# Searching the 6,249th largest score two bits at a time instead of one

## The reference, cut to what matters

```python
def _L1_ffn_ref(x, attention_mask, wr, br, w1, b1, w2, b2):
    b, s, d = x.shape                      # here 1, 12500, 256
    weights = (jnp.einsum('bsd,do->bso', x, wr) + br)[..., 0]
    k = max(1, int(CAPACITY * s))          # CAPACITY = 0.5: 6250
    kk = k - 1 if k > 1 else 1             # 6249
    _, idx = jax.lax.top_k(weights, k)
    sel_idx = idx[:, :kk]
    sel = jnp.take_along_axis(x, sel_idx[:, :, None], axis=1)
    h = jax.nn.gelu(jnp.einsum('bkd,dh->bkh', sel, w1) + b1)
    y = jnp.einsum('bkh,hd->bkd', h, w2) + b2
    y = y * jnp.take_along_axis(weights, sel_idx, axis=1)[..., None]
    processed = jnp.zeros_like(x).at[batch_idx, sel_idx].set(y)
    return processed + x
```

## Time and profile before

| | |
|---|---|
| median of 3 runs | 8393.51 us |
| lowest, highest | 8387.45, 8396.27 us |
| the profiled execution: its time | 8392.08 us |
| the profiled execution: its span | 8390.3 us |
| busy PE / PE weight loads / DVE / ACT / POOL | 77% / 58% / 42% / 23% / 46% |
| mean granted TensorE clock | 0.868 of full speed |
| instructions | 109,810 |

### The profile page before, as it was taken

How to read it: one execution, slowest core, us unless ns; L and a number is a source line. 1 busy time by engine, 2 the same in 40 slices (tenths; PEclk the granted TensorE clock), 3 DMA queues, 4 the chain that set the end, 5 groups by cost and what they waited for, 6 DMA issues and landing times. The chain is left out here.

```text
span 8390.3 us, 109810 instructions
## 1 busy us (share of the span) xinstructions
PE 6473.1 (77%) x28541; PEld 4831.1 (58%) x28542; DVE 3545.2 (42%) x8238; ACT 1915.5 (23%) x4350; POOL 3823.0 (46%) x3997
## 2 busy tenths in 40 slices
PE   3797887778876899576578888785488877798699
PEld 2555555555555677463266666564366665577677
DVE  3211123333333322333345555555666655577620
ACT  1123430000011122121022222221012334465121
POOL 1567777777774000067777777774200000000231
PEclk9898878898886799758889998897799999899599
DMA  5776769999982100267677777775477766564520
GB/s 162 253 243 225 226 230 343 346 340 344 337 303 87 53 20 21 53 209 238 218 246 243 240 240 240 238 242 153 142 237 238 225 204 195 181 203 160 175 73 17
DMA packets 604940, 1708.05 MB, mean 204 GB/s; under 512 B 109370, under 2 KB 334479, under 8 KB 515140
## 3 DMA queue, kind: packets, MB, share of 16 engines
q1 hardware_dynamic: 338260, 981.33, 34.0%
q0 software_dynamic: 190752, 655.07, 24.6%
q10 hardware_dynamic: 75764, 69.93, 2.8%
HBM read 1084.38 MB, written 624.00 MB: 204 GB/s over the span
## 5 line engine op out<-in xcount | busy, mean ns | idle before, releaser
L723 POOL DMA_INDIRECT rows_ring<-h_rows,src_idx x1660 | 1726.3, 1040 | 653.0 <-issue 505.3
L1839 POOL DMA_INDIRECT x_sb<-xn_rows,src_tile x1563 | 1526.5, 977 | 470.7 <-issue 449.0
L2610 PE MATMUL sums_ps_sum<-x_sb,sums_weighted 128*125 x4124 | 1003.5, 400 | 264.1 <-DVE sums_weighted L2574 162.2
L816 PE MATMUL agg_ps_sum<-agg_rows,agg_sel_w 128*128 128x257 f32 x3080 | 996.6, 472 | 271.0 <-DMA agg_rows<-edge_rows 185.2
L2610 PEld LDWEIGHTS sums_ps_sum<-x_sb,sums_weighted 128*125 128x125 f32 x4124 | 786.0, 196 | 481.5 <-issue 352.2
L2574 DVE SCALAR_TENSOR_TENSOR sums_weighted<-x_sb 128x125 f32 x2062 | 720.0, 349 | 539.8 <-PE sums_ps_sum L2610 385.4
L816 PEld LDWEIGHTS agg_ps_sum<-agg_rows,agg_sel_w 128*128 128x128 f32 x3080 | 532.4, 217 | 513.3 <-issue 375.1
L792 DVE TENSOR_TENSOR agg_sel<-iota,dst_item 128x1280 bf16<-128x1280 f32 x166 | 249.9, 1505 | 878.5 <-PE agg_ps_sum L817 875.3
L2540 POOL DMA_INDIRECT node_tops<-tops,last_edge x98 | 93.1, 950 | 1127.1 <-DMA x_sb<-row_lots 1109.7
L2642 ACT ACTIVATE sums_z<-sums_ps_sum 125x257 f32<-125x257 f32 x500 | 193.0, 386 | 864.2 <-PE sums_ps_sum L2610 764.0
L2131 PE MATMUL mix_ps_h<-mix_x1t,mix_w 128*128 128x256 f32 x1600 | 384.4, 396 | 0.7 <-ACT mix_x1t L2193 0.7
(11 more groups left out here) (555 smaller groups left out, 11085.8 us busy)
## 6 DMA issues: line engine op xcount, KB each, us to landing
row_lots<-x_sb SPq DMA_DIRECT2D x195, 1048.0 KB
x_sb<-row_lots SPq DMA_DIRECT2D x195, 1048.0 KB
edge_rows<-rows_ring POOLq DMA_DIRECT2D x154, 1290.0 KB
agg_rows<-edge_rows SPq DMA_DIRECT2D x154, 1290.0 KB
sums<-sums_z ACTq DMA_DIRECT2D x500, 125.5 KB
fin_z<-sums SPq DMA_DIRECT2D x97, 642.5 KB, 3.8
xn_turned<-norm_xt SPq DMA_DIRECT2D x150, 256.0 KB, 2.0
rows_ring<-h_rows,src_idx POOLq DMA_INDIRECT x1660
```

The lines of the kernel that those rows point to most:

```text
L723: pool.indirect_dma_start(self.ring[:, s, i, :], None, self.table, bass.IndirectOffsetOnAxis(g.src_idx[:, item:item + 1], 0)).then_inc(sel ...
L816: pe.matmul(ps[:, bass.ds(off, W)], sel_w[:, u, j, :], tiles[:, j, 0:W], start=False, stop=False, skip_group_check=True)
L1839: pool.indirect_dma_start(self.ring[:, s, i, :], None, g.xn_rows, bass.IndirectOffsetOnAxis(g.src_tile[:, tile:tile + 1], 0)).then_inc(sel ...
L2610: pe.matmul(ps[0:M, bass.ds(bank, SW)], weighted[:, s + j, :, :].rearrange("p n w -> p (n w)"), rows[:, bass.ds(off, SW)], start=False, st ...
```

## The change

The search takes two bits a step. Three candidates (digit 1, 2 and 3 at the two bits under test) are compared in a row, each with its own column of `cnt`; one matmul sums the three columns; the largest digit whose total is at least `need` is or-ed into `cur`. The steps go from 31 to 16 (the last has one bit left: its digits are 0, 1 and 1). The conditional copy and the bare semaphore increment go; a reduction to the maximum and one more "or" come in. The candidates of the next step are formed at the end of a step, so the first ones are a copy ahead of the loop, and three constants are set instead of one. The diff, its declarations cut:

```diff
-        hit = ph.sb("hit", [P, TILES])
-        cnt = ph.sb("cnt", [P, 1])
+        hit = ph.sb("hit", [P, 3, TILES])
+        cnt = ph.sb("cnt", [P, 3])
...
-        BITS = 31
+        STEPS = 16
...
-                with pe.Fori(0, BITS + 2) as k:
-                    pe.wait_ge(counted, k + 1)
+                pe.wait_ge(counted, 1)
+                pe.matmul(ps_c[:, 0:1], g.ones[:, :], cnt[:, 0:1], start=True, stop=True).then_inc(summed, 1)
+                with pe.Fori(0, STEPS) as k:
+                    pe.wait_ge(counted, 3 * k + 4)
                     pe.matmul(ps_c[:, :], g.ones[:, :], cnt[:, :], start=True, stop=True).then_inc(summed, 1)
...
-                done(dve.memset(bit[:, :], 1 << (BITS - 1)))
+                for d in range(3):
+                    done(dve.memset(digit[:, d:d + 1], (d + 1) << 29))
                 done(dve.memset(cur[:, :], 0))
+                done(dve.tensor_copy(cand[:, :], digit[:, :]))
                 base = n.n
 
-                with dve.Fori(0, BITS) as k:
-                    m = Count(base + 3 * k)
-                    dve.tensor_tensor(cand[:, :], cur[:, :], bit[:, :], ALU.bitwise_or).then_inc(step, 1)
+                with dve.Fori(0, STEPS) as k:
+                    m = Count(base + 5 * k)
+                    for d in range(3):
+                        dve.tensor_scalar(hit[:, d, :], um[:, :], cand[:, d:d + 1].bitcast(F32), 0.0, ALU.is_ge, ALU.add,
+                                          accum_out=cnt[:, d:d + 1]).then_inc(counted, 1)
+                    dve.wait_ge(summed, k + 2)
+                    dve.scalar_tensor_tensor(won[:, :], ps_c[:, :], need[:, 0:1], digit[:, :], ALU.is_ge, ALU.mult).then_inc(step, 1)
                     dve.wait_ge(step, m.up())
-                    dve.tensor_scalar(hit[:, :], um[:, :], cand[:, :].bitcast(F32), 0.0, ALU.is_ge, ALU.add, accum_out=cnt[:, :]).then_inc(counted, 1)
-                    dve.wait_ge(summed, k + 2)
-                    dve.tensor_scalar(ok[:, :], ps_c[:, :], need[:, 0:1], None, ALU.is_ge).then_inc(step, 1)
+                    dve.tensor_reduce(best[:, :], won[:, :], AX, ALU.max).then_inc(step, 1)
+                    dve.tensor_scalar(digit[:, :], digit[:, :], 2, None, ALU.logical_shift_right).then_inc(step, 1)
+                    dve.wait_ge(step, m.up(2))
+                    dve.tensor_tensor(cur[:, :], cur[:, :], best[:, :], ALU.bitwise_or).then_inc(step, 1)
                     dve.wait_ge(step, m.up())
-                    dve.sem_inc(ok_seen, 1)
-                    dve.copy_predicated(cur[:, :], ok[:, :], cand[:, :])
-                    dve.tensor_scalar(bit[:, :], bit[:, :], 1, None, ALU.logical_shift_right).then_inc(step, 1)
+                    dve.tensor_tensor(cand[:, :], cur[:, :].to_broadcast([P, 3]), digit[:, :], ALU.bitwise_or).then_inc(step, 1)
                     dve.wait_ge(step, m.up())
```

More of the change, by code:

```diff
@@ L2895, in select @@
     with phase(nc, "sel") as ph:
-        loaded, counted, summed, step, rank_done, ok_seen, stored = (
-            ph.sem(s) for s in ("loaded", "counted", "summed", "step", "rank_done", "ok_seen", "stored"))
+        loaded, counted, summed, step, rank_done, stored = (
+            ph.sem(s) for s in ("loaded", "counted", "summed", "step", "rank_done", "stored"))
         br = ph.sb("br", [P, 1])
@@ L2900, in select @@
         um = ph.sb("um", [P, TILES])
-        hit = ph.sb("hit", [P, TILES])
-        cnt = ph.sb("cnt", [P, 1])
+        hit = ph.sb("hit", [P, 3, TILES])
+        cnt = ph.sb("cnt", [P, 3])
         sign = ph.sb("sign", [P, 1])
         need = ph.sb("need", [P, 1])
-        ok = ph.sb("ok", [P, 1], I32)
-        bit = ph.sb("bit", [P, 1], I32)
+        won = ph.sb("won", [P, 3], I32)
+        best = ph.sb("best", [P, 1], I32)
+        digit = ph.sb("digit", [P, 3], I32)
         cur = ph.sb("cur", [P, 1], I32)
-        cand = ph.sb("cand", [P, 1], I32)
+        cand = ph.sb("cand", [P, 3], I32)
         thr = ph.sb("thr", [P, 1])
@@ L2913, in select @@
         run = ph.sb("run", [P, TILES])
-        ps_c = ph.psum("c", [P, 1])
+        ps_c = ph.psum("c", [P, 3])
         ps_in = ph.psum("in", [P, TILES])
         ps_tot = ph.psum("tot", [P, TILES])
-        BITS = 31
+        STEPS = 16
         with nc.Block() as block:
@@ L2929, in _ @@
             def _(pe):
-                with pe.Fori(0, BITS + 2) as k:
-                    pe.wait_ge(counted, k + 1)
+                pe.wait_ge(counted, 1)
+                pe.matmul(ps_c[:, 0:1], g.ones[:, :], cnt[:, 0:1], start=True, stop=True).then_inc(summed, 1)
+                with pe.Fori(0, STEPS) as k:
+                    pe.wait_ge(counted, 3 * k + 4)
                     pe.matmul(ps_c[:, :], g.ones[:, :], cnt[:, :], start=True, stop=True).then_inc(summed, 1)
-                pe.wait_ge(counted, BITS + 3)
+                pe.wait_ge(counted, 3 * STEPS + 2)
+                pe.matmul(ps_c[:, 0:1], g.ones[:, :], cnt[:, 0:1], start=True, stop=True).then_inc(summed, 1)
+                pe.wait_ge(counted, 3 * STEPS + 3)
                 pe.matmul(ps_in[:, :], g.upper[:, :], eq[:, :], start=True, stop=True)
@@ L2949, in _ @@
                 done(dve.tensor_tensor(w[:, :], w[:, :], g.maskbias[:, :], ALU.add))
-                dve.tensor_scalar(hit[:, :], w[:, :], 0.0, 0.0, ALU.is_ge, ALU.add, accum_out=cnt[:, :]).then_inc(counted, 1)
+                dve.tensor_scalar(hit[:, 0, :], w[:, :], 0.0, 0.0, ALU.is_ge, ALU.add, accum_out=cnt[:, 0:1]).then_inc(counted, 1)
                 dve.wait_ge(summed, 1)
-                done(dve.tensor_scalar(sign[:, :], ps_c[:, :], float(KEEP), None, ALU.is_ge))
+                done(dve.tensor_scalar(sign[:, :], ps_c[:, 0:1], float(KEEP), None, ALU.is_ge))
                 done(dve.tensor_scalar(need[:, :], sign[:, :], float(2 * KEEP - NODES - 1), float(NODES - KEEP + 1), ALU.mult, ALU.add))
@@ L2974, in _ @@
                     dve.wait_ge(step, m.up())
-                n = Count(base + 3 * BITS)
+                n = Count(base + 5 * STEPS)
                 done(dve.tensor_scalar(thr[:, :], cur[:, :].bitcast(F32), sign[:, 0:1], None, ALU.mult))
                 dve.tensor_scalar(eq[:, :], w[:, :], thr[:, 0:1], None, ALU.is_equal)
-                dve.tensor_scalar(gt[:, :], w[:, :], thr[:, 0:1], 0.0, ALU.is_gt, ALU.add, accum_out=cnt[:, :]).then_inc(counted, 1)
-                dve.wait_ge(summed, BITS + 2)
@@ L2980, in _ @@
-                done(dve.tensor_scalar(need[:, :], ps_c[:, :], -1.0, float(KEEP), ALU.mult, ALU.add))
+                dve.tensor_scalar(gt[:, :], w[:, :], thr[:, 0:1], 0.0, ALU.is_gt, ALU.add, accum_out=cnt[:, 0:1]).then_inc(counted, 1)
+                dve.wait_ge(summed, STEPS + 2)
+                done(dve.tensor_scalar(need[:, :], ps_c[:, 0:1], -1.0, float(KEEP), ALU.mult, ALU.add))
                 dve.sem_inc(counted, 1)
```

## The result

The changed kernel takes 8361.82 us in the median of nine runs (8341.08 to 8370.81), the kernel before 8384.15 in nine runs beside it (8375.49 to 8396.27). The ratio is 0.997 with a 95% interval of 0.996 to 0.998, so 22.3 us were gained where 24.4 were forecast. The time itself, though, lies 0.2 us under the lower end of the stated range, because the kernel before is not at the 8393.51 from which I started, but 9 us lower: three of its nine runs are the three I started from, and they are among the four slowest.

The account below looks back on a forecast made before the run. VectorE's chain of small dependent instructions was taken to bound `select`: sixteen steps of 2.77 us, with 0.45 ahead of the loop, make 44.6 instead of 69.01, so 24.4 off 8393.51 gives 8369.1 us; range 8362 to 8379.

Parts of the forecast that it names:

- (a): Three counts and their reads, up to the matmul: overlapping without waits, 0.245 us per extra count, 0.87 in all.
- (f): Second "or" at the end of a search step, 0.16 us, then wait and loop end 0.39: 0.55.
- (c): Comparison and product `won` in a search step, up to the reduction: 0.26 us, upper bound 0.37.
- (d): Reduction to the maximum and overlapping shift, up to the first "or": 0.26 us, upper bound 0.60.
- rival 1: VectorE doesn't overlap in the search loop: 0.36 us per extra count, shift after the reduction; gain 18.8 us; chance 0.09.
- Ahead of the loop: Before the search loop: two more constants at 0.13 us each and one copy of about 0.19, 0.45 in all.
- same 446 us: The phase after `select` should take as long as before, from its first instruction to the kernel's end.
- rival 3: TensorE's clock doesn't rise in the next phase: up to 15 us more per group of 256 picked rows; chance 0.03.
- 2: Search-loop waits dearer than 0.04 us, three at 0.11 more, and a reduction at 0.42: gain 15.0 us; chance 0.13.
- 4: The output store, not the search, ends the `select` phase; the gain of 24.4 us is not touched; chance 0.01.
- lower bound of a step: Shortest search step forecast: 2.65 us, with which 26.4 us go.
- Faster by over 0.2%: Whole kernel below 8376.7 us, given a chance of 0.84.

## Why the prediction was right and where it was not

- **What bounds.** Right. VectorE's chain sets the phase's end; the store has landed 18 us before it, and the run with 25 steps shows that the length of the search goes into the time in full.
- **Terms (a) to (f).** Right, each within 0.01 us, and the choice within each pair of bounds too: the runs with an added wait or increment give (a) 0.36 instead of 0.24 a count, (c) 0.36 instead of 0.26, (d) 0.39 instead of 0.26, within 0.01 of what I had written as the bound of (a) and (c) and as rival 1's price of (d). In (d) two errors of 0.01 to 0.02 cancel, which is luck: the shift starts 0.07 behind the reduction and lasts 0.16, where 0.08 and 0.14 were written.
- **Ahead of the loop.** 0.45 was forecast for two more constants and the copy. From the first constant to the loop's first instruction there are 0.86 us (7862.22 to 7863.08) instead of 0.39 (7868.37 to 7868.76): 0.47.
- **The sum.** 24.4 forecast, 24.6 in select's own stretch, less 0.4 in the last phase. The medians beside each other give 22.3, 21.4 and 24.0.
- **The last phase's "same 446 us".** Nearly: it took 0.1 to 1.3 us more in the nine traces with a shorter select, and 446.4 in the three with the old length. "The next phase starts from the same level before and after, with the same matmuls" is true, and yet the clock rises 0.1 to 2.7 us later. This is rival 3's mechanism at a small part of the 15 us a group that it was priced at; the clock is at 1.00 for the rest of the phase.
- **The rivals.** 3 came only as this trace of itself. 1 was priced rightly (0.24 and 0.12 us a step measured with its waits put in, 0.23 and 0.12 written) but is not what the chain does. Of 2, the 0.11 is what a bare increment costs (0.10) and not a wait, which is 0.04 here, and the reduction takes 0.16 and not 0.42. 4 was excluded by the landing of the store.
- **The step that failed** is the last sum, from the gain to a time. "It lies 1.4 below the median of the three runs (8393.51), so beside the median it is 8369.1", with "half the spread of the runs, 4.4" for the lower end. The three runs of before had a median 9.4 us above that of the nine to which they belong, and their spread of 8.8 us was taken for the kernel's, where the nine have 20.8. The medians of the same kernel are 8384.15, 8386.32 and 8400.16 in the three comparisons, and single executions go from 8371.05 to 8419.18, 48 us, more than the whole gain. So two terms were mis-sized: the base by 9.4 us, and the spread at 4.4 where half of the nine's is 10.4. The time came 7.3 us below the forecast: 9.4 from the base, less 2.1 because 22.3 were gained and not 24.4. With 10.4 for the spread the range would have begun at about 8357 and held the changed kernel's median in all three comparisons (8361.82, 8378.72, 8362.27). That the first lies 0.2 us outside, and not just inside, is chance; the base was mis-sized either way.
- **The lower bound of a step** is also added up wrongly: with (d) at 0.20 and the gaps at 0.03 it is 2.67 to 2.69, depending on how many gaps are counted, and not 2.65. That makes a gain of about 26.0 at most and not 26.4, and a lower end of 8363.
- **"Faster by over 0.2%"** came by the medians in all three comparisons (0.27 to 0.31%), but the intervals reach down to 0.18 to 0.2%, so it is only just clear of the line that was drawn.

## What to carry to other kernels

A chain of small dependent instructions can be forecast to a hundredth of a microsecond an instruction from the start-to-start distances of the same chain, if one also asks of each gap which instruction without data of its own (a wait, an increment, a loop's end) stands in it; such gaps are also what is left to take. The forecast of the difference is then much surer than that of the time: a change of 0.3% has to be stated with the spread that the base has from execution to execution and from one comparison to the next, and three runs side by side don't show it. Where that spread is larger than the gain, a run that puts the changed piece back to its old length, and a table of the phases from several traces, tell more than another median.

## What the runs showed that was not expected

In this chain a wait on the own semaphore between two counts of 100 columns costs 0.12 us, a bare increment 0.10 and the end of a loop 0.36, against 0.24 for a whole further count of 128x100 numbers. Ahead of select the same instructions took between 7846.8 and 7885.9 us; of the 39 us between these two, 10 lie ahead of the first aggregation and 15 in it. And the clock of the last phase rose up to 2.7 us later than before with the same matmuls behind the same barrier, which took back up to 1.3 us of the gain.
